# Four-layer convolution and attention kernel: tokens in raster order from the load on, and the mixer's stage order rewritten with three images in a turn

## Chip, cores and metric

The kernel runs on one NeuronCore of a Trainium2 chip. The metric is device time in microseconds of one execution; the time of a kernel is the median of several executions. TensorE (PE) has two clocks in these records, 1.2 and 2.4 GHz; a granted clock of 1.00 is 2.4 GHz.

## Reference

Sixteen images of 16 x 16 tokens with 96 channels pass through four layers: a window attention with an MLP, a convolutional mixer with an MLP, an attention over all 256 tokens with a quantised feed-forward part, a causal attention with a mixture of experts. Everything is float32. The change touches how tokens are laid out in the first layer, and the order of the work in the mixer of the second:

```python
h = _layernorm(x, n1_g, n1_b)
p = h @ w_in + b_in                                   # 96 -> 192 channels
local = depthwise 3x3 convolution of p
lr, rl = _ema_scan(local, axis=2), _ema_scan(local, axis=2, reverse=True)
tb, bt = _ema_scan(local, axis=1), _ema_scan(local, axis=1, reverse=True)
mixed = 0.25 * (lr + rl + tb + bt) + local
mixed = _layernorm(mixed, on_g, on_b)                 # over 192 channels
x = x + (mixed @ w_out + b_out)
```

The four scans are linear over the 256 tokens of an image, so the kernel does them, with the sum, as one product with a constant 256 x 256 matrix (`mixer`).

## The kernel before

X, the residual stream, stays in SBUF as 32 tiles of 128 tokens x 96 channels, two tiles an image. A tile is half an image (8 rows of 16 tokens). Until the mixer, the 128 tokens of a tile lie in window order: first the 64 tokens of the left 8 x 8 window, then those of the right one. From the mixer on they lie in raster order. The stages follow one another, each a block with one instruction stream for each engine, and semaphores between the streams. An engine runs its stream strictly in order, so the order in which the code calls its helpers is the order of the work.

**Load.** `x_loads` (line 344) issues for each group of four images and each window column eight DMAs of 8 partitions each; 64 in all, 8 of them on ScalarE's queue ahead of the first constants (`first`, line 384, of which the identity is the last) and the 16 loads of the bias table (line 386), 56 on SP's queue (line 350) ahead of the weights of the later layers (`k.late`, line 444). GpSimd's line 367 and TensorE's line 378 wait for the constants, and the first attention starts behind them.

**First attention.** TensorE transposes the normalised tiles (line 480), so that tokens become columns, and at the end transposes the outputs back (line 541), both in window order; the projection gives X in the same order.

**Mixer** (`conv_mixer`). Image n passes these steps; names are those of the functions in the code:
- tokens: GpSimd normalises (lines 156 to 165), TensorE transposes (L872), ScalarE copies out with scale and bias in two ACTIVATEs that also turn window order into raster order (L944);
- widen: 96 -> 192 channels (L879); ScalarE writes the result into two padded grids (L953);
- convolution: channels 0 to 127 on VectorE as nine dependent multiply-adds ("taps", L1019 for the first and L1022), channels 128 to 191 on TensorE (taps, L888), copied out by ScalarE as `acc1` (L968);
- conv_t: TensorE transposes both back to tokens (L901, L902), ScalarE copies out as `loc` (L976);
- mix: the product with the 256 x 256 matrix into bank 7 (L844);
- norm2: VectorE takes mean and variance (L984, L989), GpSimd the reciprocal root (L825, L827), VectorE normalises into Z (norm2b, L996);
- back: TensorE transposes Z (L854), ScalarE copies out with scale and bias as `zT` (zt, L936);
- out: TensorE projects 192 -> 96 (L865) and adds X itself in raster order by a product with a permutation matrix (`perm`, L863) into the same bank;
- residual: VectorE copies that to X (L178) and takes the statistics for the next MLP (L187, L193).

In turn n the engines run:
- TensorE: a warming product (`keep_warm`, L129, a bf16 product whose result is not used), tokens(n+1), out(n-2), mix(n-1), taps(n), widen(n+1), a warming product, back(n-1), a warming product, conv_t(n);
- ScalarE: tokens(n+1), acc1(n), grid(n+1), zt(n-1), loc(n);
- VectorE: taps 0 to 4 of n, residual(n-2), tap 5, norm2(n-1), taps 6 and 7, norm2b(n-1), tap 8;
- GpSimd: the normalisation for n+2, the reciprocal root for n-1.

conv_t(n) waits for all nine taps of n on VectorE, mix(n) for loc(n), norm2(n) for mix(n).

Of the kernel before, what the change touches and what calls it, by code (L numbers as in the profile page):

```python
# [22 lines left out]
ALU = mybir.AluOpType  # L23
# [3 lines left out]
P = 128  # L27
# [147 lines left out]
def add_new(dve, k, s, n, count, new, replace=False):  # L175

    x = tiles_of(k.X, n * count, count)
    (dve.tensor_copy(x, new) if replace else dve.tensor_tensor(x, x, new, ALU.add)).then_inc(s["x"], 1)  # L178
# [24 lines left out]
def add_and_stats(dve, k, s, n, count, new, replace=False):  # L203
    add_new(dve, k, s, n, count, new, replace)
    statistics(dve, k, s, n, count)
# [8 lines left out]
def setup(k, bank, a):  # L214
# [83 lines left out]
    k.perm = weight("perm", [P, P], a["perm"])  # L298
# [46 lines left out]
    def x_loads(eng, g, wx):  # L345

        for r in range(WS):
            p0 = wx * WTOK + r * WS
            src = a["x"].rearrange("b (y i) (v c) d -> v i c (b y) d", i=WS, c=WS)[wx, r]
            eng.dma_start(k.X[p0:p0 + WS, 8 * g:8 * g + 8, :], src[:, 8 * g:8 * g + 8, :]).then_inc(s[f"x{g}"], 16)  # L350

    def sync(sp):
        x_loads(sp, 0, 0)
        for g in range(1, 4):
            for wx in range(2):
                x_loads(sp, g, wx)
        sp.wait_ge(s["ones"], 1)
# [23 lines left out]
    def scalar(act):  # L381
        x_loads(act, 0, 1)
        for dst, src in first:
            act.dma_start(dst, src, allow_slow_non_contiguous=True).then_inc(s["w"], 16)
        for dst, src in table_loads:
            act.dma_start(dst, src, allow_slow_non_contiguous=True).then_inc(s["wr"], 16)
        act.wait_ge(s["w"], 16 * len(first))
        act.wait_ge(s["wr"], 16 * len(table_loads))
# [13 lines left out]
def image_stats(dve, k, s, i):  # L402

    dve.wait_ge(s[f"x{i // 4}"], 16 * 2 * WS)
    after(dve, s["mv"], i)
    for t in range(2):
        last = dve.bn_stats(k.stats[:, 6 + t, :], k.X[:, 2 * i + t, None, :])
    last.then_inc(s["bn"], 1)
    dve.wait_ge(s["bn"], i + 1)
    for t in range(2):  # L410
        last = dve.bn_aggr(k.MV[:, 2 * i + t, :], k.stats[:, 6 + t, :])
    last.then_inc(s["mv"], 1)


def window_attention(k, bank, begin):
# [3 lines left out]
    with ExitStack() as ctx:  # L419
# [19 lines left out]
        with nc.Block() as block:  # L439
# [33 lines left out]
            def _(pe):  # L473
                def tokens_t(n):

                    pe.wait_ge(s["y"], n + 1)
                    after(pe, s["hT"], n)
                    after(pe, s["x"], n - 4)
                    for t in range(2):
                        last = pe.transpose(bank[0][0:C, t * P:(t + 1) * P], k.Y[n % 2][:, t, :], k.ident[:])  # L480
                    last.then_inc(s["T"], 1)
# [55 lines left out]
                def outputs_t(n):  # L537
                    pe.wait_ge(s["a"], 2 * n + 2)
                    pe.wait_ge(s["hT"], min(n + 5, IMAGES))
                    for t in range(2):  # L540
                        last = pe.transpose(bank[0][0:C, t * P:(t + 1) * P], A[n % 2][:, t, :], k.ident[:])
                    last.then_inc(s["oT"], 1)
# [233 lines left out]
def raster(t, y):  # L776

    return t.rearrange("p (y i v c) -> p y v i c", y=2, i=WS, v=2)[:, y]


def conv_mixer(k, bank):

    nc = k.nc
    s = k.sems("cm", LN_SEMS + "z T hT in p taps acc1 conv ct loc mix bn2 ag2 va2 rs2 z2 zT zTe out diag init")
    with ExitStack() as ctx:
# [11 lines left out]
        v2, r2 = sb("v2", [P, 2, 1]), sb("r2", [P, 2, 1])  # L797
        Z = sb("z", [P, 2, CI])
        ZT = sb("zT", [P, 2, 2, P])

        with nc.Block() as block:
            @block.gpsimd
            def _(pool):
# [34 lines left out]
            def _(pe):  # L838
                def mix(n):
                    pe.wait_ge(s["loc"], n + 1)  # L840
                    after(pe, s["z2"], n)
                    for t in range(2):
                        for j in range(2):
                            last = pe.matmul(bank[7][:, t * CI:(t + 1) * CI], k.mixer[:, j, t * P:(t + 1) * P], loc[:, j, :],  # L844
                                             start=(j == 0), stop=(j == 1))
# [47 lines left out]
                def conv_t(n, slot):  # L893

                    keep_warm(pe, k, bank[4][:])
# [13 lines left out]
                for n in range(IMAGES + 2):  # L909
                    slot = n % 2  # L910
                    keep_warm(pe, k, bank[4][:])
# [12 lines left out]
                    if n < IMAGES:  # L924
                        conv_t(n, slot)

            @block.scalar
            def _(act):
# [11 lines left out]
                def tokens(n, slot):  # L940
                    act.wait_ge(s["T"], n + 1)
                    after(act, s["in"], n - 1)
                    for y in range(2):
                        last = act.activation(raster(k.hT[slot][:, 0:TOK], y), bank[0][0:C, y * P:(y + 1) * P].rearrange("p (v i c) -> p v i c", v=2, i=WS),  # L944
                                              ACT.Identity, bias=k.b3[:], scale=k.g3[:])
                    last.then_inc(s["hT"], 1)
# [14 lines left out]
                for n in range(IMAGES + 1):  # L961
                    slot = n % 2
                    if n + 1 < IMAGES:
                        tokens(n + 1, 1 - slot)
                    if n < IMAGES:
# [5 lines left out]
                    if n >= 1:  # L971
                        zt(n - 1)
# [6 lines left out]
            def _(dve):  # L979
                def norm2(n):  # L980
                    dve.wait_ge(s["mix"], n + 1)
                    after(dve, s["va2"], n)
                    for t in range(2):
                        last = dve.bn_stats(st2[:, t, :], bank[7][:, t * CI:(t + 1) * CI])  # L984
# [7 lines left out]
                def norm2b(n):  # L992
                    dve.wait_ge(s["rs2"], n + 1)
                    after(dve, s["zT"], n)
                    for t in range(2):
                        last = dve.tensor_scalar(Z[:, t, :], bank[7][:, t * CI:(t + 1) * CI], ag2[:, t, 0:1], r2[:, t, :], ALU.subtract, ALU.mult)  # L996
                    last.then_inc(s["z2"], 1)

                def residual(n):
                    dve.wait_ge(s["out"], n + 1)  # L1000
                    dve.wait_ge(s["xb"], n + 1)
                    add_and_stats(dve, k, s, n, 2, bank[6][:, 0:2 * C].rearrange("p (t c) -> p t c", t=2), replace=True)

                def body(n, slot, first, last):
# [18 lines left out]
                in_turn(IMAGES, body)  # L1023
                residual(IMAGES - 2)
                norm2(IMAGES - 1)
                norm2b(IMAGES - 1)
# [1172 lines left out]
def constants():  # L2199
# [7 lines left out]
    tok = np.arange(TOK).reshape(2, WS, 2, WS).transpose(0, 2, 1, 3).reshape(-1)  # L2207
# [4 lines left out]
        "perm": (tok[0:P, None] == np.arange(P)[None, :]).astype(f),  # L2212
# [23 lines left out]
```

## Time and profile before

| | us |
|---|---|
| median of 3 runs | 1274.22 (1272.11 to 1274.35) |
| the profiled execution | 1279.13 |
| its span | 1277.4 |

| engine | busy us | share of the span |
|---|---|---|
| TensorE matmul | 1150.9 | 90% |
| TensorE weight load | 786.9 | 62% |
| VectorE | 722.3 | 57% |
| ScalarE | 513.6 | 40% |
| GpSimd | 386.5 | 30% |

The profile is one execution recorded by the hardware; spans count from its first instruction. Busy shares are means over stages with different limits: the first attention runs from about 20 to 160 us, its MLP to 219, the mixer to 378, the second MLP to 435, the rest to the end. TensorE's granted clock is 0.954 over the whole.

### The profile page before, as it was taken

What the parts mean: (1) busy time and instruction counts of PE and PEld (TensorE: products, weight loads), DVE (VectorE), ACT (ScalarE), POOL (GpSimd) and SP (SyncE); (2) the same over time, 40 slices, a digit from 0 to 9 for tenths busy, and PEclk for the clock granted to TensorE, in tenths of its full rate; (3) what the DMA queues carried; (4) which work ended last, traced back from release to release, by engine and by line L of the source; (5) the groups of instructions that cost most, each with busy time, mean ns of one, the idle gap of its engine ahead of it and who ended that gap; (6) DMA issues with size and microseconds to landing.
All of it is one profiled execution on the core that took longest, in us unless ns stands there. A gap on an engine that the chain in (4) does not pass through costs nothing. (4 is left out here: it accounts for less than half of the span.)

```text
span 1277.4 us, 23732 instructions
## 1 busy us (share of the span) xinstructions
PE 1150.9 (90%) x8911; PEld 786.9 (62%) x8911; DVE 722.3 (57%) x2035; ACT 513.6 (40%) x839; POOL 386.5 (30%) x584
## 2 busy tenths in 40 slices
PE   4999988999979799999999996788898887999998
PEld 2677655666646566767676664465445444577776
DVE  3899633777743266666666675475556556333232
ACT  1666532444413244333433330545344322445543
POOL 3666463544336311110101111434001000263522
PEclk9999999899989899999999997888899997999999
DMA  4500000000000000000000000000000000000000
GB/s 89 97 18 2 2 1 0 1 1 1 1 1 1 1 1 1 1 1 1 1 1 1 1 1 1 0 1 1 2 2 2 1 2 1 1 13 7 13 7 13
DMA packets 28923, 9.38 MB, mean 7 GB/s; under 512 B 26961, under 2 KB 28816, under 8 KB 28816
## 3 DMA queue, kind: packets, MB, share of 16 engines
q1 hardware_dynamic: 25760, 7.02, 2.7%
q8 instruction: 69, 1.13, 0.4%
q10 hardware_dynamic: 3056, 0.92, 0.3%
q14 instruction: 38, 0.31, 0.1%
HBM read 6.36 MB, written 1.57 MB: 6 GB/s over the span
## 5 line engine op out<-in xcount | busy, mean ns | idle before, releaser
L156 POOL TENSOR_TENSOR ln_v<-MV,eps 128x2 f32<-128x2 f32 (+3 forms) x81 | 16.4, 202 | 420.5 <-PE bank L1144 245.8
L1206 ACT ACTIVATE fa_e<-bank 128x1024 f32<-128x1024 f32 x64 | 65.5, 1024 | 158.5 <-PE bank L1114 158.5
L2009 PEld LDWEIGHTS bank<-e_w,ex_G 128*128 128x128 f32 x768 | 90.6, 192 | 14.4 <-issue 14.1
L2124 DVE SCALAR_TENSOR_TENSOR X<-bank,ex_L,X 128x96 f32<-128x96 f32 x128 | 31.7, 310 | 114.5 <-PE bank L2009 108.8
L1258 DVE TENSOR_REDUCE fa_z<-bank 128x4 f32<-128x1024 f32 x64 | 77.9, 1216 | 26.3 <-PE bank L1096 24.7
L2001 PE MATMUL bank<-hT,e_w 96*128 96x512 f32 x192 | 91.3, 612 | 0.0
L2009 PE MATMUL bank<-e_w,ex_G 128*128 128x96 f32 x768 | 90.0, 274 | 0.0
L2052 ACT ACTIVATE ex_G<-bank,e_b 128x512 f32<-128x512 f32 x96 | 64.4, 687 | 63.0 <-PE bank L2001 60.2
L1856 DVE TENSOR_REDUCE ca_z<-bank 128x2 f32<-128x256 f32 x96 | 48.9, 552 | 50.2 <-PE bank L1583 50.0
L1114 PE MATMUL bank<-fa_a,fa_b 64*128 64x256 f32 x512 | 73.4, 406 | 1.1 <-DVE fa_a L1265 1.1
L1127 PE MATMUL bank<-fa_e,fa_v 128*64 128x256 f32 x512 | 71.2, 400 | 1.1 <-ACT fa_e L1206 1.1
L159 POOL TENSOR_TENSOR ln_r<-ln_v,minus_half 128x2 f32<-128x2 f32 (+3 forms) x81 | 71.8, 887 | 0.0
L1774 ACT ACTIVATE ca_e<-bank 128x768 f32<-128x768 f32 x48 | 38.9, 811 | 80.7 <-PE bank L1583 80.7
L1022 DVE SCALAR_TENSOR_TENSOR cm_acc<-cm_g,k_conv,cm_acc 128x256 f32<-128x256 f32 x128 | 64.7, 505 | 3.0
L1096 PE MATMUL bank<-fa_b,fa_a 64*128 64x256 f32 x512 | 66.0, 376 | 0.1
L1955 POOL TENSOR_TENSOR ex_tmp<-e_b,ex_L 128x384 f32<-128x384 f32 x8 | 6.7, 835 | 190.5 <-DVE ex_L L2112 190.5
L1114 PEld LDWEIGHTS bank<-fa_a,fa_b 64*128 64x128 f32 x512 | 44.7, 189 | 29.4 <-issue 24.6
L178 DVE TENSOR_TENSOR X<-X,bank 128x192 f32<-128x192 f32 (+2 forms) x56 | 23.7, 429 | 67.3 <-PE bank L730 43.0
L468 POOL TENSOR_TENSOR wa_s<-wa_s,wa_mx 128x768 f32<-128x768 f32 x32 | 47.1, 1473 | 46.9 <-DVE wa_mx L666 46.9
L1569 PE MATMUL bank<-ca_b,ca_a 16*128 16x256 f32 (+1 forms) x384 | 48.0, 369 | 14.3 <-DVE ca_a L1865 13.8
L163 POOL TENSOR_TENSOR Y<-Y,ln_r 128x192 f32<-128x192 f32 (+3 forms) x81 | 56.2, 694 | 10.9
L1265 DVE TENSOR_TENSOR fa_a<-fa_a,bank 128x256 f32<-128x256 f32 x64 | 26.9, 421 | 56.3 <-PE bank L1104 56.3
(252 smaller groups left out, 2620.3 us busy)
## 6 DMA issues: line engine op xcount, KB each, us to landing
out_tokens<-X SPq DMA_DIRECT2D x8, 192.0 KB, 2.1
X<-in_x SPq DMA_DIRECT2D x56, 24.0 KB
e_w<-in_L_ffn_w SPq DMA_DIRECT2D x2, 576.0 KB
bias0r<-in_L_conv_rpb_table ACTq DMA_DIRECT2D x16, 24.0 KB
m0w<-in_L_conv_mlp_w SPq DMA_DIRECT2D x2, 144.0 KB
m1w<-in_L_conv_w SPq DMA_DIRECT2D x2, 144.0 KB
f_w<-in_L_ffn_W SPq DMA_DIRECT2D x2, 142.5 KB
mixer<-in_mixer SPq DMA_DIRECT2D x1, 256.0 KB
```

The lines of the kernel that those rows point to most:

```text
L159: pool.tensor_tensor(r, v, k.minus_half[:, 0:count, :], ALU.pow).then_inc(s["rstd"], 1)
L163: pool.tensor_tensor(y, y, r.broadcast_to([P, count, C]), ALU.mult).then_inc(s["y"], 1)
L1022: dve.scalar_tensor_tensor(out=o, in0=src, scalar=kk, in1=o, op0=ALU.mult, op1=ALU.add).then_inc(s["conv"], 1)
L1096: last = pe.matmul(bank[b + i][:, c * TOK:(c + 1) * TOK], A[n % 2][rows, p, c * P:(c + 1) * P], B[n % 2][rows, p, :], start=True, stop=True)
L1114: last = pe.matmul(bank[b + i][:, c * TOK:(c + 1) * TOK], B[n % 2][rows, p, c * P:(c + 1) * P], A[n % 2][rows, p, :], start=True, stop=True)
L1127: last = pe.matmul(bank[4 + v % 2][64 * i:64 * i + 64, 0:TOK], V[n % 2][:, c, 2 * p + i, :], E[v % 2][:, i, c, :], start=(c == 0), stop=(c ...
L1206: act.activation(E[v % 2][:], k.banks[:, b:b + 2, :].rearrange("p i (c q) -> p i c q", c=2), ACT.Exp).then_inc(s["exp"], 1)
L1258: dve.tensor_reduce(Z[v % 2][:].rearrange("p c (i d) -> p i c d", i=2)[:, :, :, D2], k.banks[:, b:b + 2, :].rearrange("p i (c q) -> p i c ...
L1856: last = dve.tensor_reduce(dst, k.banks[:, 2 * p:2 * p + 2, c * P:(2 * c + 1) * P], AX.X, ALU.max, negate=True)
L2001: pe.matmul(bank[v % NB][:], k.ew1[:, e, j * P:(j + 1) * P], k.hT[slot][:], start=True, stop=True).then_inc(s["up"], 1)
L2009: last = pe.matmul(bank[4 + e % 2][:, t * C:(t + 1) * C], G[e % 2][:, j, t * P:(t + 1) * P], k.ew2[:, e, j, :], start=(j == 0), stop=(j == ...
L2052: act.activation(G[e % 2][:, j, :], bank[(KH * e + j) % NB][:], ACT.Gelu, bias=k.eb1[:, e, j:j + 1]).then_inc(s["gelu"], 1)
```

## The change

- X is loaded with one DMA an image, in raster order; 2 of the 16 are issued by ScalarE, 14 by SP. The transposes of the first attention write their columns in window order, those of its output read in window order and write in raster order. The permutation matrix and its two products go; the residual is added by VectorE.
- In the mixer the normalisation after the mixing moves from VectorE to ScalarE (`normalised`, two ACTIVATEs with scale and bias from columns); GpSimd makes the bias in two more small operations. The result of the mixing has two banks (7 and 4) by turns. back, zt and out of an image come a turn later than before; residual comes in the third turn after the taps.
- The order within a turn changes on all engines, the last turn runs two turns after the last taps, and the warming products of the mixer go.

```diff
-    def x_loads(eng, g, wx):
-        for r in range(WS):
-            p0 = wx * WTOK + r * WS
-            src = a["x"].rearrange("b (y i) (v c) d -> v i c (b y) d", i=WS, c=WS)[wx, r]
-            eng.dma_start(k.X[p0:p0 + WS, 8 * g:8 * g + 8, :], src[:, 8 * g:8 * g + 8, :]).then_inc(s[f"x{g}"], 16)
+    def x_load(eng, image):
+        src = a["x"].rearrange("b (y i) w d -> (i w) (b y) d", i=WS)
+        eng.dma_start(k.X[:, 2 * image:2 * image + 2, :], src[:, 2 * image:2 * image + 2, :]).then_inc(s[f"x{image // 4}"], 16)
     def sync(sp):
-        x_loads(sp, 0, 0)
-        for g in range(1, 4):
-            for wx in range(2):
-                x_loads(sp, g, wx)
+        for image in (0, 2) + tuple(range(4, IMAGES)):
+            x_load(sp, image)
     def scalar(act):
-        x_loads(act, 0, 1)
+        for image in (1, 3):
+            x_load(act, image)
...
-                        last = pe.transpose(bank[0][0:C, t * P:(t + 1) * P], k.Y[n % 2][:, t, :], k.ident[:])
+                        windows = bank[0][0:C, t * P:(t + 1) * P].rearrange("p (v i c) -> p i v c", v=2, i=WS)
+                        last = pe.transpose(windows, k.Y[n % 2][:, t, :], k.ident[:])
...
-                        last = pe.transpose(bank[0][0:C, t * P:(t + 1) * P], A[n % 2][:, t, :], k.ident[:])
+                        rows = bank[0][0:C, t * P:(t + 1) * P].rearrange("p (i v c) -> p v i c", i=WS, v=2)
+                        last = pe.transpose(rows, A[n % 2][:, t, :], k.ident[:])
...
+        mixed = (bank[7], bank[4])
...
                     pool.tensor_tensor(v2[:], ag2[:, :, 1:2], k.eps[:, 0:2, :], ALU.add).then_inc(s["va2"], 1)
-                    pool.wait_ge(s["va2"], n + 1)
+                    pool.tensor_scalar(m2[:, :, 0], ag2[:, :, 0], -1.0, 0.0, ALU.mult, ALU.add).then_inc(s["va2"], 1)
+                    pool.wait_ge(s["va2"], 2 * n + 2)
                     pool.tensor_tensor(r2[:], v2[:], k.minus_half[:, 0:2, :], ALU.pow).then_inc(s["rs2"], 1)
+                    pool.wait_ge(s["rs2"], n + 1)
+                    pool.tensor_tensor(o2[:], m2[:], r2[:], ALU.mult).then_inc(s["of2"], 1)
...
                 def mix(n):
                     pe.wait_ge(s["loc"], n + 1)
-                    after(pe, s["z2"], n)
+                    after(pe, s["z2"], n - 1)
...
                 def out(n):
                     pe.wait_ge(s["zTe"], n + 1)
                     after(pe, s["x"], n)
-                    pe.wait_ge(s["xb"], n + 1)
                     for t in range(2):
-                        o = bank[6][:, t * C:(t + 1) * C]
-                        pe.matmul(o, k.perm[:], k.X[:, bass.ds(n * 2 + t, 1), :], start=True, stop=False)
                         for j in range(2):
-                            last = pe.matmul(o, ZT[0:part[j], j, t, :], k.wout[0:part[j], j, :], start=False, stop=(j == 1))
+                            last = pe.matmul(bank[6][:, t * C:(t + 1) * C], ZT[0:part[j], j, t, :], k.wout[0:part[j], j, :],
+                                             start=(j == 0), stop=(j == 1))
...
                 for n in range(IMAGES + 2):
                     slot = n % 2
-                    keep_warm(pe, k, bank[4][:])
                     if n + 1 < IMAGES:
                         tokens(n + 1, 1 - slot)
                     if n >= 2:
-                        out(n - 2)
+                        back(n - 2)
+                    if n < IMAGES:
+                        taps(n, slot)
                     if 1 <= n <= IMAGES:
                         mix(n - 1)
-                    if n < IMAGES:
-                        taps(n, slot)
                     if n + 1 < IMAGES:
                         widen(n + 1, 1 - slot)
-                    if 1 <= n <= IMAGES:
-                        back(n - 1)
+                    if n >= 2:
+                        out(n - 2)
                     if n < IMAGES:
                         conv_t(n, slot)
...
+                def normalised(n):
+                    act.wait_ge(s["of2"], n + 1)
+                    after(act, s["zT"], n)
+                    for t in range(2):
+                        last = act.activation(Z[:, t, :], mixed[n % 2][:, t * CI:(t + 1) * CI], ACT.Identity, bias=o2[:, t, :], scale=r2[:, t, :])
+                    last.then_inc(s["z2"], 1)
...
-                for n in range(IMAGES + 1):
+                for n in range(IMAGES + 2):
                     slot = n % 2
+                    if n >= 2:
+                        normalised(n - 2)
                     if n + 1 < IMAGES:
                         tokens(n + 1, 1 - slot)
+                    if n >= 2:
+                        zt(n - 2)
...
                     if n + 1 < IMAGES:
                         widened(n + 1, 1 - slot)
-                    if n >= 1:
-                        zt(n - 1)
...
                     for tap in range(9):
-                        if tap == 5 and n >= 2:
-                            residual(n - 2)
-                        if tap == 6 and not first:
+                        if tap == 1 and n >= 3:
+                            residual(n - 3)
+                        if tap == 4 and not first:
                             norm2(n - 1)
-                        if tap == 8 and not first:
-                            norm2b(n - 1)
```

The two `keep_warm` lines in front of back and conv_t go as well, `norm2b` goes, ScalarE's tokens become one ACTIVATE of 256 columns, and after the last turn VectorE runs residual(13), norm2(15), residual(14), residual(15).

## Rows read from the trace of the kernel before

**Rows 1.** Windows: busy time of each engine in a stretch, granted clock, DMA share, GB/s.

```profile
core 0: us, PE busy (x) PEld busy (x) DVE busy (x) ACT busy (x) POOL busy (x), PEclk, DMA share, GB/s
233.00:300.00 67.00, 60.94 (x386) 44.21 (x384) 53.78 (x152) 28.06 (x67) 27.16 (x52) 1.00 0.01 1
```

**Rows 2.** Timeline of one turn of the mixer; start, duration, engine, line.

```profile
300.37 0.87 DVE L996 TENSOR_SCALAR cm_z<-bank,cm_ag,cm_r 128x192 f32<-128x192 f32 x2 [0.60 <-POOL cm_r L827]
...
301.14 0.48 DVE L1022 SCALAR_TENSOR_TENSOR cm_acc<-cm_g,k_conv,cm_acc 128x256 f32<-128x256 f32 x1
301.29 0.39 PEld L854 LDWEIGHTS bank<-ident,cm_z 128*128 128x128 f32 x4 [1.52 <-DVE cm_z L996]
...
301.78 0.14 PEld L901 LDWEIGHTS bank<-ident,cm_acc 128*128 128x128 f32 x1
301.92 2.38 DVE L1022 SCALAR_TENSOR_TENSOR cm_acc<-cm_g,k_conv,cm_acc 128x256 f32<-128x256 f32 x4
...
302.90 0.47 ACT L976 ACTIVATE cm_loc<-bank 128x384 f32<-128x384 f32 x1
303.05 0.30 PEld L863 LDWEIGHTS bank<-X,perm 128*128 128x128 f32 x2
...
305.05 1.57 PE L844 MATMUL bank<-cm_loc,mixer 128*128 128x192 f32 x8
...
306.55 1.52 PE L888 MATMUL bank<-cm_g,cm_diag 128*64 128x256 f32 x12
306.67 0.62 DVE L984 BATCH_NORM_STATS2 cm_st<-bank 128x6 f32<-128x192 f32 x2
...
307.56 0.45 DVE L1022 SCALAR_TENSOR_TENSOR cm_acc<-cm_g,k_conv,cm_acc 128x256 f32<-128x256 f32 x1
```

**Rows 3.** Timeline: conv_t of images 0 and 15, taps without GpSimd beside them.

```profile
232.25 0.14 PEld L901 LDWEIGHTS bank<-ident,cm_acc 128*128 128x128 f32 x1 [0.96 <-DVE cm_acc L1022]
...
354.74 2.05 DVE L1022 SCALAR_TENSOR_TENSOR cm_acc<-cm_g,k_conv,cm_acc 128x256 f32<-128x256 f32 x4
...
363.12 0.14 PEld L901 LDWEIGHTS bank<-ident,cm_acc 128*128 128x128 f32 x1
```

**Rows 4.** Groups by form, 240 to 366 us; busy us, mean ns, idle before.

```profile
L944 ACT ACTIVATE hT<-bank,w_b,w_g 96x128 f32<-96x128 f32 x26 | 10.3, 452 | 0.0
L936 ACT ACTIVATE cm_zT<-bank,on_b,on_g 128x256 f32<-128x256 f32 x15 | 8.5, 566 | 7.2 <-PE bank L854 7.2
```

**Rows 5.** Timeline of the mixer's tail, after the last mixing.

```profile
370.99 1.11 PE L854 MATMUL bank<-ident,cm_z 128*128 128x128 f32 x4 [2.81 <-DVE cm_z L996]
...
373.21 0.74 PE L863 MATMUL bank<-X,perm 128*128 128x96 f32 x2 [0.68 <-ACT cm_zT L936]
...
374.97 0.74 PE L863 MATMUL bank<-X,perm 128*128 128x96 f32 x2
...
376.85 0.36 DVE L178 COPY X<-bank 128x192 f32<-128x192 f32 x1 [5.92 <-PE bank L865]
```

**Rows 6.** Timeline of the kernel's start; the queues' own rows are the issues.

```profile
0.74 3.05 ACTq L350 DMA_DIRECT2D X<-in_x  x8
0.75 19.60 SPq L350 DMA_DIRECT2D X<-in_x  x56
...
8.70 0.45 ACTq L384 DMA_DIRECT2D ident<-in_ident  x1
...
12.86 0.37 POOL L367 TENSOR_SCALAR bv_wide<-ones,w_bv 96x128 f32<-96x128 f32 x1 [9.80 <-DMA ident<-in_ident]
```

**Rows 7.** Taps in the mixer's first turn (timeline); windows of 3 us in later stages.

```profile
227.10 2.83 PE L888 MATMUL bank<-cm_g,cm_diag 128*64 128x256 f32 x12
...
910.00:913.00 3.00, 1.44 (x20) 0.93 (x19) 1.50 (x3) 0.81 (x1) 0.00 (x0) 1.00 0.01 3
913.00:916.00 3.00, 3.00 (x36) 1.47 (x32) 1.10 (x3) 0.81 (x1) 0.00 (x0) 0.62 0.00 0
...
1038.00:1041.00 3.00, 1.70 (x21) 1.06 (x21) 1.48 (x4) 0.81 (x1) 0.00 (x0) 1.00 0.00 0
```

More of the change, by code:

```diff
@@ L172, in next_first_step, with add_new @@
     normalise(pool, k, s, steps, count, k.Y[0][:, 0:count, :], bias, steps, 0)
-def add_new(dve, k, s, n, count, new, replace=False):
+def add_new(dve, k, s, n, count, new):
     x = tiles_of(k.X, n * count, count)
-    (dve.tensor_copy(x, new) if replace else dve.tensor_tensor(x, x, new, ALU.add)).then_inc(s["x"], 1)
+    dve.tensor_tensor(x, x, new, ALU.add).then_inc(s["x"], 1)
 def statistics(dve, k, s, n, count, unrolled=True):
@@ L200, in statistics, with add_and_stats @@
     dve.tensor_copy(tiles_of(k.MV, n * count, count), k.aggr[:, 0:count, :]).then_inc(s["mv"], 1)
-def add_and_stats(dve, k, s, n, count, new, replace=False):
-    add_new(dve, k, s, n, count, new, replace)
+def add_and_stats(dve, k, s, n, count, new):
+    add_new(dve, k, s, n, count, new)
     statistics(dve, k, s, n, count)
@@ L297, in setup @@
     k.bout = row("b_out", a["L1_conv_b_out"])
-    k.perm = weight("perm", [P, P], a["perm"])
     k.mixer = weight("mixer", [P, 2, TOK], a["mixer"].rearrange("(j p) t -> p j t", p=P))
@@ L402, in image_stats @@
 def image_stats(dve, k, s, i):
-    dve.wait_ge(s[f"x{i // 4}"], 16 * 2 * WS)
+    dve.wait_ge(s[f"x{i // 4}"], 16 * 4)
     after(dve, s["mv"], i)
@@ L773, in _ @@
                 residual(steps - 1)
-def raster(t, y):
-    return t.rearrange("p (y i v c) -> p y v i c", y=2, i=WS, v=2)[:, y]
 def conv_mixer(k, bank):
     nc = k.nc
-    s = k.sems("cm", LN_SEMS + "z T hT in p taps acc1 conv ct loc mix bn2 ag2 va2 rs2 z2 zT zTe out diag init")
+    s = k.sems("cm", LN_SEMS + "z T hT in p taps acc1 conv ct loc mix bn2 ag2 va2 rs2 of2 z2 zT zTe out diag init")
     with ExitStack() as ctx:
@@ L796, in conv_mixer @@
         st2, ag2 = sb("st2", [P, 2, 6]), sb("ag2", [P, 2, 2])
-        v2, r2 = sb("v2", [P, 2, 1]), sb("r2", [P, 2, 1])
+        v2, r2, m2, o2 = (sb(f"{name}2", [P, 2, 1]) for name in "vrmo")
         Z = sb("z", [P, 2, CI])
         ZT = sb("zT", [P, 2, 2, P])
+        mixed = (bank[7], bank[4])
         with nc.Block() as block:
@@ L840, in mix @@
                     pe.wait_ge(s["loc"], n + 1)
-                    after(pe, s["z2"], n)
+                    after(pe, s["z2"], n - 1)
                     for t in range(2):
                         for j in range(2):
-                            last = pe.matmul(bank[7][:, t * CI:(t + 1) * CI], k.mixer[:, j, t * P:(t + 1) * P], loc[:, j, :],
+                            last = pe.matmul(mixed[n % 2][:, t * CI:(t + 1) * CI], k.mixer[:, j, t * P:(t + 1) * P], loc[:, j, :],
                                              start=(j == 0), stop=(j == 1))
@@ L893, in conv_t @@
                 def conv_t(n, slot):
-                    keep_warm(pe, k, bank[4][:])
                     pe.wait_ge(s["conv"], 9 * (n + 1))
@@ L910, in _ @@
                     slot = n % 2
-                    keep_warm(pe, k, bank[4][:])
                     if n + 1 < IMAGES:
@@ L942, in tokens @@
                     after(act, s["in"], n - 1)
[L943 to L946, printed above, removed]
+                    act.activation(k.hT[slot][:, 0:TOK], bank[0][0:C, 0:TOK], ACT.Identity, bias=k.b3[:], scale=k.g3[:]).then_inc(s["hT"], 1)
+                def normalised(n):
[4 more added lines that the diff above has]
+                    last.then_inc(s["z2"], 1)
                 def widened(n, slot):
@@ L981, in norm2 @@
                     dve.wait_ge(s["mix"], n + 1)
-                    after(dve, s["va2"], n)
+                    after(dve, s["va2"], 2 * n)
                     for t in range(2):
-                        last = dve.bn_stats(st2[:, t, :], bank[7][:, t * CI:(t + 1) * CI])
+                        last = dve.bn_stats(st2[:, t, :], mixed[n % 2][:, t * CI:(t + 1) * CI])
                     last.then_inc(s["bn2"], 1)
@@ L990, in norm2 @@
                     last.then_inc(s["ag2"], 1)
[L992 to L997, printed above, removed]
                 def residual(n):
@@ L1001, in residual @@
                     dve.wait_ge(s["xb"], n + 1)
-                    add_and_stats(dve, k, s, n, 2, bank[6][:, 0:2 * C].rearrange("p (t c) -> p t c", t=2), replace=True)
+                    add_and_stats(dve, k, s, n, 2, bank[6][:, 0:2 * C].rearrange("p (t c) -> p t c", t=2))
                 def body(n, slot, first, last):
@@ L1023, in _ @@
                 in_turn(IMAGES, body)
+                residual(IMAGES - 3)
+                norm2(IMAGES - 1)
                 residual(IMAGES - 2)
-                norm2(IMAGES - 1)
-                norm2b(IMAGES - 1)
                 residual(IMAGES - 1)
@@ L2206, in constants @@
     mixer = np.eye(TOK) + 0.25 * (np.kron(eye, scan) + np.kron(scan, eye))
-    tok = np.arange(TOK).reshape(2, WS, 2, WS).transpose(0, 2, 1, 3).reshape(-1)
     return {
@@ L2211, in constants @@
         "stack2": np.tile(np.eye(CI - P, dtype=f), (2, 1)),
-        "perm": (tok[0:P, None] == np.arange(P)[None, :]).astype(f),
         "headmask": (np.arange(C)[:, None] // D0 % (H0 // 3) == np.arange(H0 // 3)[None, :]).astype(f),
```

## Prediction

> **What bounds the kernel now.** The window view comes first, stage by stage: all of the arithmetic that the change touches lies in the mixer, and there TensorE is busy 60.9 of 67 us and VectorE 53.8, the clock at 2.4 GHz [rows 1]. With both that full, shares decide nothing; the turn has to be read in the timeline, engine against engine. The reader should follow one loop in it [rows 2]. The last tap of image n ends on VectorE at 301.62; 0.16 us later TensorE starts the transposes of the convolution (conv_t, 301.78); ScalarE copies them out until 303.37 (loc); TensorE meanwhile does the tokens of the next image and the output projection, and at 305.05 starts the mixing, which ends at 306.62; VectorE starts the statistics at 306.67 and is back at its taps at 307.56. Behind that come two taps, GpSimd's reciprocal root (VectorE waits 0.60 us for it), VectorE's normalisation (0.87) and the last tap, and the next conv_t. Nothing in this loop has slack over about 1 us. conv_t starts fifteen turns apart at 232.25 and 363.12: 130.87 us, 8.72 us a turn [rows 3].
>
> **What the change moves in the turn.** In turn n TensorE now runs: tokens(n+1), back(n-2), taps(n), mix(n-1), widen(n+1), out(n-2), conv_t(n). ScalarE runs: z(n-2) (the normalisation, two ACTIVATEs), tokens(n+1), zt(n-2), acc1(n), the grid of n+1, loc(n). VectorE runs: tap 0, residual(n-3), taps 1 to 3, statistics of n-1, taps 4 to 8. I lay it out from conv_t(n-1) at time 0, with the durations of before.
>
> - loc(n-1) ends at 303.37 - 301.78 = 1.59 [rows 2]. z(n-2) stands behind it in ScalarE's queue, though its inputs were ready a turn ago. 128x192 with scale and bias from columns does not occur; the nearest forms are 96x128 at 452 ns and 128x256 at 566 ns [rows 4], so 0.51 each. One ACTIVATE starts about 0.1 before the one in front ends (two of 0.45 take 0.80), so the pair takes 0.92 and ends at 1.59 - 0.10 + 0.92 = 2.41. Bounds of the pair: 0.80 (two of the smaller form) and 1.02 (two of the larger).
> - TensorE has its tokens done at about 1.1 and waits. back(n-2) starts at 2.45 and gives way after 0.39 of weight loads [rows 2]: taps(n) start at 2.84. They take 1.52, of which, as between mix and taps now, 0.07 overlaps: mix(n-1) starts at 4.29 and ends at 4.29 + 1.57 = 5.86 [rows 2].
> - VectorE's tap 0, residual and taps 1 to 3 need about 0.4 + 1.3 + 1.65, so it stands at the statistics from 3.2 on, and waits some 2.7 us for the mixing. Statistics start at 5.91 and hold it for 307.56 - 306.67 = 0.89: 6.80.
> - Five taps remain. Four took 2.38 beside GpSimd's work and 2.05 without it [rows 2, 3], 0.51 to 0.60 each; five cost 2.56 to 2.98, taken 2.75: 9.55. conv_t(n) starts 0.16 later: **9.71 us a turn**, with 9.2 to 10.1 as bounds when all the small terms fall one way.
>
> All of it is one closed chain (conv_t, loc, z, back, taps, mix, statistics, five taps), so work taken off beside it brings nothing. VectorE loses z, 0.87 a turn, and gains about 0.1 (adding in place of copying): cover, as it now waits 2.7. TensorE loses the two permutation products (out is now 2.00 us for six products, a third of them permutations) and all three or four warming products: out ends at 5.86 + 1.0 + 1.35 = 8.2, and TensorE then waits 1.5 for the taps. GpSimd gains two operations of some 0.2 to 0.35, beside a wait of several us. The tokens' one ACTIVATE for two (0.3 less) is beside the wait for taps. The second bank for the mixing removes a wait that nobody stood at.
>
> The first turn has no z and no back: tokens done at 1.1, taps at 1.2, mix ends at 4.22, then 0.05 + 0.89 + 2.75 + 0.16 give 8.07. Fourteen more at 9.71 are 135.9. Together 144.0 against 130.87: **+13.1 us** (9.2 a turn: +5.8; 10.1: +18.5).
>
> **Tail.** Now 376.85 - 363.12 = 13.73 from the last conv_t to the last residual [rows 3, 5]. After: mix(15) behind back(14) without taps between ends at 4.41; statistics to 5.3; GpSimd's four small operations about 1.6; z(15) 0.92: 7.8; back at 1.2 GHz 1.11; zt 1.0; out twice 1.76 [rows 5] less its third for the permutation, 2.4: 12.4. **-1.3.** The head of the stage gains 0.3 from the tokens.
>
> **Load.** ScalarE issues eight X loads in 3.05 us before the constants; the identity is issued at 8.70 and GpSimd, TensorE and everything behind wait for it until 12.86 [rows 6]. Now there are two X loads. At 0.38 each the other six are 2.3 us. The loads are four times as large, and SP's 14 are out by about 6 us rather than at 20.35 [rows 6], so more is in flight when the identity travels. The nearest row for that is the identity itself, 4.1 us from issue to use under the present traffic; bounds: another 1.5 us off that, or 4 us on top. Taken: **-2.0**, range -3.5 to +2. SP's weight loads start some 14 us earlier and are needed after 160 us: nothing. The Trainium skill (Trainium Kernel Development and Optimization, Key Constraints) says that loads of the SP and ACT queues run on the same 16 engines and interleave, so that several issuers save issue time only; by it the transfer gains nothing and the saving is the 2.3 us of issue at most. No row separates the two.
>
> In the first attention the transposes write their columns in window order; that they cost more appears in no row. A transpose takes a slot of 0.1 us (0.39 for four [rows 2]); 64 of them at double price would be 6 us. Taken at nothing: the number of columns is the same.
>
> The Trainium skill (ScalarE: Activation LUTs, What ACT_TABLE_LOAD costs) gives an ACTIVATE 186 ns and 0.833 ns an element, 93 ns more for each column operand, and an overlap of 93 ns between neighbours. For z that is 532 ns, a pair of 0.97 us: an estimate from the page, against VectorE's 0.87 now. It speaks against moving z, and by it the fifteen turns would be 0.7 us longer still. The rows that it can be held to agree: 566 measured for 128x256 against 585.
>
> **Clock.** From the end of out (8.2) to the next taps (9.71 + 2.84 = 12.55) TensorE has 4.3 us with only conv_t, tokens and back in them, some 1.4 us of short operations, and the warming products that stood there are gone. The rows show what such thin stretches were followed by, and it is not always the same: after 3 us with TensorE busy 1.44 came a spell at 1.2 GHz, through 3 us with 1.70 it stayed at 2.4 [rows 7], and after the 2.81 us wait in the tail back came at 1.2 [rows 5]. So this cost is open. Taps take 2.83 at 1.2 GHz and 1.52 at 2.4 [rows 7, 2]; with a piece of the mixing a fall costs 1.3 to 1.7 us of the chain. The clock comes back once the dense part of the turn has run, so I take a fall in one turn of three, between never and always: 5 times 1.4, **+7** (0 to 22).
>
> **Sum.** 13.1 - 1.3 - 0.3 - 2.0 + 7 = +16.5. The profiled execution took 1279.1 (span 1277.4), so it would take 1295.6; it lies 4.9 above the median of 1274.2, and against the median I forecast **1290**.
>
> **The rivals.**
>
> *The clock holds.* The loop is the same and no fall is paid: +9.5, 1283.7 (1279 to 1287 by the turn's bounds). For it: in the mixer now TensorE waits over 1 us each turn and the clock never falls [rows 1, 2]; against: warming products fill those waits.
>
> *The clock falls every turn.* 14 times 1.6: +22 in place of +7, 1306. If it fell and stayed, TensorE's whole part of the chain (conv_t, back, taps, mix, 4.2 us) would double: 14 times 4.2, near 1340. Against that: the dense part has brought the clock back each time, as at 913 [rows 7].
>
> *Faster: the wait for z is not paid.* Place: back(n-2) on TensorE. Price: if z were there when TensorE comes (1.1 and not 2.45), the mixing would end 1.35 sooner and the turn be 8.36; 8.07 + 14 x 8.36 = 125.1, -5.8, with tail, head and load -9.4 and no low clock: 1265. It decides from a mixing that ends before 4.9 after conv_t, where the turn is 8.75. For it: z's inputs are ready early and it has a bank of its own. Against it: z can't pass loc in ScalarE's queue, and loc needs conv_t.
>
> *It comes out even.* A turn at 9.2, no low clock and the full gain of the load: +5.8 - 1.6 - 3.5, 1275.
>
> **How the numbers follow.** Forecast 0.45; clock holds 0.27; falls every turn 0.11, stays low 0.05; even 0.05; faster 0.07. The range leaves out the faster, the even and the stay-low case: 1278 to 1308. A measurement can tell about 0.2%, 2.5 us, from no change: slower 0.88, same 0.05, faster 0.07.
>
> **What would show it.** In the profile of after: conv_t starts 9.7 us apart (10 to 10.5 where the clock fell); VectorE waits about 2.7 us a turn for the mixing before the statistics, and hardly at all for GpSimd or out; TensorE waits about 1.3 us for z before back and 1.5 for the taps before conv_t; identity in use at about 10.8; granted clock in the mixer below 1.00 in some slices. I am wrong on the main term if VectorE reaches the statistics after the mixing has ended, or if turns are under 9.2 us.

## The result and the profile after

| | before | after |
|---|---|---|
| median, us (4 runs each) | 1273.16 (1269.46 to 1274.35) | 1311.91 (1310.65 to 1312.31) |
| span of the profiled execution, us | 1277.4 | 1310.5 |
| its TensorE clock | 0.954 | 0.932 |
| conv_t of image 0, of image 15, us | 232.25, 363.12 | 227.64, 395.27 |
| between the two, us | 130.87 | 167.63 |
| of it at 1.2 GHz, us | 0 | 64.9 in 14 spells |

The change makes the kernel slower: ratio 1.0308, 95% interval 1.0284 to 1.0332. That is 38.7 us on the medians, where 16.5 was forecast; 1311.91 lies above the range as well. The direction was right, and so was the closed loop that the prediction laid out; the term for the clock was much too small.

The two spans differ by 33.1 us, and four stretches make them up: the start until conv_t(0) -4.6, the fifteen turns +36.8, the tail +0.5, everything behind +0.4. (The rest of the 38.7: the profiled execution of before lay 6.0 above the median of its four runs, that of after 0.4.) The stages behind the mixer took 893 to 901 us in the twelve kernels shown here, with the same code in them, so below the turns are compared first and whole times second.

The mixer in the view of waits of after, 226 to 400 us (who waits for whom: us in total, times, longest):

```profile
DVE cm_st L982 <- PE bank L841: 69.1, 15, 6.0
...
PEld bank L894 <- DVE cm_acc L1011: 25.7, 16, 3.1
...
PE bank L894 <- DVE cm_acc L1011: 22.6, 16, 2.7
...
PE bank L850 <- ACT cm_z L941: 19.8, 15, 1.5
```

All three waits that the prediction named are there. TensorE waits 1.3 us a turn for z (L850) and 1.5 for the taps (L894); VectorE waits for the mixing (L982), but 4.6 a turn and not 2.7. The timeline of one turn of after shows why:

```profile
292.12 0.14 PEld L894 LDWEIGHTS bank<-ident,cm_acc 128*128 128x128 f32 x1 [1.46 <-DVE cm_acc L1011]
...
292.95 0.49 ACT L974 ACTIVATE cm_loc<-bank 128x384 f32<-128x384 f32 x1 [2.13 <-PE bank L895]
...
293.46 0.91 ACT L941 ACTIVATE cm_z<-bank,cm_o,cm_r 128x192 f32<-128x192 f32 x2
...
295.06 2.83 PE L882 MATMUL bank<-cm_g,cm_diag 128*64 128x256 f32 x12
...
297.82 1.80 PE L841 MATMUL bank<-cm_loc,mixer 128*128 128x192 f32 x8
...
299.66 0.63 DVE L982 BATCH_NORM_STATS2 cm_st<-bank 128x6 f32<-128x192 f32 x2 [4.34 <-PE bank L841]
...
300.56 2.54 DVE L1011 SCALAR_TENSOR_TENSOR cm_acc<-cm_g,k_conv,cm_acc 128x256 f32<-128x256 f32 x5
...
303.14 0.14 PEld L894 LDWEIGHTS bank<-ident,cm_acc 128*128 128x128 f32 x1 [1.46 <-DVE cm_acc L1011]
```

The loop is the forecast one: conv_t 292.12, loc, z until 294.37, back, taps at 295.06, mixing at 297.82, statistics at 299.66, five taps, conv_t at 303.14. But the taps take 2.83 us and the mixing 1.80, against 1.52 and 1.57 in [rows 2]. Windows over the same turn give the clock (the last three numbers are clock, DMA share, GB/s):

```profile
289.00:292.00 3.00, 1.83 (x11) 1.33 (x9) 2.75 (x10) 1.30 (x3) 2.14 (x6) 1.00 0.00 0
292.00:294.40 2.40, 1.00 (x8) 0.75 (x8) 2.17 (x9) 1.43 (x4) 2.27 (x4) 1.00 0.00 0
294.40:297.90 3.50, 3.47 (x17) 1.70 (x17) 0.89 (x2) 1.44 (x3) 0.12 (x1) 0.57 0.02 5
...
299.60:303.10 3.50, 2.25 (x13) 1.70 (x11) 3.19 (x10) 1.30 (x3) 2.22 (x6) 1.00 0.00 0
```

TensorE stands for 1.46 us, does 1.00 us of short transposes in 2.4, and the clock then falls to 1.2 GHz under back and the taps, which are on the chain. It is back by the end of the mixing, the two waits come again, and it falls again. Over 67 us of the mixer, where [rows 1] has TensorE busy 60.94 at 1.00:

```profile
233.00:300.00 67.00, 50.59 (x255) 35.66 (x256) 35.23 (x100) 26.77 (x59) 27.16 (x54) 0.80 0.00 1
```

The turns after the first take 10.8 to 12.6 us in place of 8.72 (nine of 10.8 to 11.1, five of 12.2 to 12.6; in the long ones the mixing is wholly at 1.2 GHz too, 2.5 to 2.7 us).

### The profile page after: what moved, and what is told of

Same layout as the page of the kernel before. It is cut to its first block and busy times, and to the rows that moved or that the text cites. A ratio compares the mean times of both kernels' runs of the same rounds, so it can differ in the third digit from the quotient of the medians.

```text
span 1310.5 us, 23469 instructions
## 1 busy us (share of the span) xinstructions
PE 1155.4 (88%) x8797; PEld 789.9 (60%) x8797; DVE 707.7 (54%) x2003; ACT 525.5 (40%) x855; POOL 397.6 (30%) x616
## 3 DMA queue, kind: packets, MB, share of 16 engines
HBM read 6.29 MB, written 1.57 MB: 6 GB/s over the span
## 5 line engine op out<-in xcount | busy, mean ns | idle before, releaser
L178 DVE TENSOR_TENSOR X<-X,bank 128x192 f32<-128x192 f32 (+2 forms) x72 | 29.1, 409 | 74.3 <-PE bank L728 43.0
L163 POOL TENSOR_TENSOR Y<-Y,ln_r 128x192 f32<-128x192 f32 (+3 forms) x81 | 56.3, 695 | 10.9
L157 POOL TENSOR_TENSOR Y<-X,MV 128x192 f32<-128x192 f32 (+5 forms) x81 | 58.2, 718 | 0.0
```

## The experiments

Theory A: the closed chain costs about 9 us by itself, and the rest is the clock, which falls in the two waits. Rivals: the clock is a side effect and the chain alone costs the whole; or the loss comes from one part of the change (z on ScalarE, raster order, the lost warming products). All edits are of the kernel after unless said. The turns come from the timelines (starts of conv_t), the ratios from 10 runs each where no other number stands, against 13 to 25 runs of before on the same chip.

### Three warming products back in their old places (e1_warm, 4 runs)

```diff
+                    keep_warm(pe, k, mixed[(n + 1) % 2][:])        # ahead of tokens
+                        keep_warm(pe, k, mixed[(n + 1) % 2][:])    # ahead of back
+                        keep_warm(pe, k, mixed[n % 2][:])          # ahead of conv_t
```

> The changed kernel with the three warming products of the old mixer put back at the same three places (ahead of tokens, of back and of conv_t), written into whichever of the two mixing banks is free. They run while TensorE waits anyway. Theory (low clock in every turn adds 1.5 us to a chain of 9.7): the clock stays at 2.4 GHz, conv_t starts fall from 11.2 to 9.7 us apart, 144 us from the first to the last in place of 168, and the kernel takes about 1288. Rival (the chain itself is longer than laid out, the clock is a bystander): 1305 to 1312, with turns over 11 us at a granted clock of 1.00, or with the clock falling in spite of the products.

Measured: 1301.9 us, 1.0222 (1.0195 to 1.0248). 154.67 us from first to last conv_t, 44.4 of it at 1.2 GHz in 11 spells. The clock was expected to stay up and the fifteen turns to take 144 us: it did not. The three turns without a fall took 9.42 to 9.43. So three products of some 0.2 us don't hold the clock, and they bring 13 us in the mixer by sparing three falls and shortening others. That they are gone is a small part of the loss; what is large is the waits that they no longer fill.

### Products until both waits are full (e6_warm_more)

```diff
+                        keep_warm(pe, k, mixed[(n + 1) % 2][:], 5)   # ahead of back
+                        keep_warm(pe, k, mixed[n % 2][:], 6)         # ahead of conv_t
```

> The changed kernel with more warming products than three: five (of 0.21 us each) ahead of back, in the wait for z, and six ahead of conv_t, in the wait for the taps. Theory (the chain at 2.4 GHz is 9.4 to 9.7 us, the rest of the changed kernel's 11.2 is low clock; three products a turn, as in the last experiment, filled too little of the waits): the clock stays at 2.4 GHz through the mixer, every turn is 9.4 to 9.7, fifteen 139 to 144, the kernel 1284 to 1290. Rival (warming products can't hold the clock here, or lengthen the chain themselves): turns of 10.2 or more, 1300.

Measured: 1278.0 us, 1.0038 (1.0014 to 1.0061), the clock at 1.00 from first to last conv_t. Its windows and one turn:

```profile
233.00:300.00 67.00, 64.06 (x389) 42.26 (x385) 43.28 (x123) 32.55 (x72) 32.02 (x63) 1.00 0.00 1
```

```profile
290.75 1.57 PE L841 MATMUL bank<-cm_loc,mixer 128*128 128x192 f32 x8
...
292.36 0.63 DVE L984 BATCH_NORM_STATS2 cm_st<-bank 128x6 f32<-128x192 f32 x2 [2.75 <-PE bank L841]
...
293.26 2.54 DVE L1013 SCALAR_TENSOR_TENSOR cm_acc<-cm_g,k_conv,cm_acc 128x256 f32<-128x256 f32 x5
...
295.85 0.14 PEld L894 LDWEIGHTS bank<-ident,cm_acc 128*128 128x128 f32 x1 [0.39 <-DVE cm_acc L1013]
...
297.18 0.91 ACT L943 ACTIVATE cm_z<-bank,cm_o,cm_r 128x192 f32<-128x192 f32 x2
...
298.15 0.66 PE L850 MATMUL bank<-ident,cm_z 128*128 128x128 f32 x4 [0.22 <-ACT cm_z L943]
```

This is the chain of the change at full clock, with no work of the kernel altered: 139.90 us, 7.47 for the first turn and 9.43 to 9.44 for all others but one. It splits the 36.8 us of after: **+9.0 for the chain, +27.7 for the clock**. That the clock is a cause and not a side effect is shown by this run: with eleven products that have no use the median is 33.9 us lower, and the turns without a fall in e1 above and e8 below take the same 9.43.

### Products in the wait for z alone (e8_warm_z_only, 4 runs)

```diff
+                        keep_warm(pe, k, mixed[(n + 1) % 2][:], 5)   # ahead of back
```

> The changed kernel with only the five products ahead of back; the wait before conv_t stays empty. If the thin stretch counts as a whole, from the end of out to the next taps, filling its second half saves most of the falls: turns near 9.5 mostly, 1288 to 1295. If the wait ahead of conv_t makes the clock fall by itself, turns stay at 10.5 to 11 and the kernel at 1300 to 1310.

Measured: 1291.5 us, 1.0147 (1.0106 to 1.0189), 37.5 us at 1.2 GHz in 11 spells, of which the first was already running when the stage began. TensorE in two turns, in the second of which the clock falls:

```profile
281.23 1.24 PE L129 MATMUL bank<-causal,identb 128*128 128x512 bf16 x5
...
289.82 0.33 PE L894 MATMUL bank<-ident,cm_acc 128*128 128x128 f32 x1 [1.30 <-DVE cm_acc L1012]
...
291.06 2.34 PE L129 MATMUL bank<-causal,identb 128*128 128x512 bf16 x5
293.20 0.82 PE L850 MATMUL bank<-ident,cm_z 128*128 128x128 f32 x4
293.95 1.52 PE L882 MATMUL bank<-cm_g,cm_diag 128*64 128x256 f32 x12
```

With only the wait for the taps open (1.30), the clock still falls, right behind conv_t; it hits the products and back, is over when the taps start, and such a turn takes 10.6 against 9.43. So the wait for the taps alone brings falls, in 10 turns. The wait for z alone was not tried with nothing else changed, but in e3 and e10 below it is the only one left, and there the clock falls in 10 turns too.

### Before without its warming products (e5_before_cold)

Edit of the kernel before: its three `keep_warm` calls in the mixer are removed.

> The kernel before with the three warming products of the mixer taken out and nothing else. If warming products are what kept the clock up in the old turn, the clock falls in some turns, and each fall costs 1 to 1.5 us: 1280 to 1290. If the old turn is dense enough by itself (its waits are 1.0 to 1.3 us in one place), the clock stays at 2.4 GHz and the kernel is within 3 us of 1274.

Measured: 1279.2 us, 1.0056 (1.0028 to 1.0083). Windows of its mixer:

```profile
228.00:260.00 32.00, 27.09 (x146) 19.77 (x146) 21.92 (x61) 13.66 (x33) 12.50 (x24) 0.84 0.01 1
260.00:300.00 40.00, 35.02 (x223) 25.84 (x224) 32.26 (x94) 15.73 (x38) 15.35 (x30) 1.00 0.00 1
```

In the profiled execution the clock falls twice (turns of 11.31 and 10.47) and then holds to the end at 8.76 a turn with no product at all. There the old order keeps the clock by its own work; without the products the fifteen turns take 3.9 us more, all at the start of the stage (medians: 5.9). Together with e1, where the clock falls in 11 turns with the three products back, this makes the lost products a small part of the falls in the new order.

### Raster order alone (e4_raster_only)

The kernel after (load, transposes, tokens in one ACTIVATE, adding in place of the permutation) with the mixer in its old order:

```diff
 # relative to before
-                    pe.wait_ge(s["xb"], n + 1)
-                        pe.matmul(o, k.perm[:], k.X[:, bass.ds(n * 2 + t, 1), :], start=True, stop=False)
```

> Raster order alone: loads, transposes, no permutation products and one ACTIVATE for the tokens as in the changed kernel, but the mixer's stage order, normalisation on VectorE and warming products as before. Theory: the load gives 2.9 us, and since out stands between conv_t and mix in the old order, the permutation products gone take 0.66 off each of fifteen turns: 1273.2 - 2.9 - 0.3 - 9.9 = 1260. Rival (the old turn has another bound right behind): the load's gain only, about 1270.

Measured: 1264.4 us, 0.9918 (0.9899 to 0.9938): this half of the change is a gain of 10.9. conv_t(0) at 228.29 (-4.0), then 8.31 a turn against 8.76, 124.91 in all (-6.0), with the clock at 1.00, and the tail 1.7 shorter. The removed permutation products and the shorter token copy lie on the old chain, and 0.45 a turn is what they cost there (0.66 had been expected). In the kernel after they stand beside the chain, where TensorE and ScalarE wait anyway, so the same 0.45 should be worth nothing; this is read from the loop, no run shows it.

### z an image earlier on ScalarE (e7_z_early)

```diff
-                    if n >= 2:
-                        normalised(n - 2)        # first in the turn, so behind loc(n - 1)
+                    if 1 <= n <= IMAGES:
+                        normalised(n - 1)        # ahead of loc(n)
```

> The changed kernel with z(n-1) placed ahead of loc(n) at the end of ScalarE's turn, in place of behind it in the next turn; TensorE's order and VectorE's stay. It is the case of the forecast's rival in which the wait for z is not paid. Theory: back follows tokens without a wait, the mixing ends near 4.5 after conv_t in place of 5.9, a turn is 8.4 us at 2.4 GHz; fifteen 125 us and 1269 for the kernel if the clock holds, 1280 to 1290 if it falls in most turns. Rival (z is not on the chain, the wait for it is only where a wait for something else shows): no change beside the changed kernel's 1312.

Measured: 1271.3 us, 0.9984 (0.9961 to 1.0007). back no longer waits, a turn without a fall takes 7.91 (8.4 expected), one with a fall 9.50 to 9.54; 8 spells, 27.3 us at 1.2 GHz, 131.69 in all. The only wait that TensorE has left is the one for the taps (view of waits, 240 to 335 us):

```profile
PE bank L894 <- DVE cm_acc L1011: 14.6, 11, 1.7
```

So the place in ScalarE's queue cost 9.43 - 7.91 = 1.5 us a turn, by one in-order position and not by more work.

### The statistics behind tap 8 (e3_stats_late)

```diff
-                        if tap == 4 and not first:
+                        if tap == 8 and not first:
```

> The changed kernel with the statistics (norm2) ahead of tap 8 in place of tap 4; TensorE's order stays. Theory: the mixing still ends near 5.9 after conv_t (2.4 GHz), but only one tap is left behind it, so conv_t is held by TensorE's own queue: 2.45 + 0.39 + 1.45 + 1.5 + 1.0 + 1.35 = 8.2 us a turn if the clock holds, 123 us for fifteen and 1267 for the kernel; with the clock falling in each turn 9.5 and 1286. Rival (the statistics' place is not what VectorE's wait costs, the low clock is): as the changed kernel, 1305 or more.

Measured: 1277.4 us, 1.0031 (1.0008 to 1.0055). VectorE does four more taps before it waits for the mixing: 8.07 without a fall, mostly 9.59 to 9.66 with one, 134.36 in all, 34.1 us at 1.2 GHz in 10 spells. Here TensorE waits for z alone (same view and stretch), and the clock falls all the same:

```profile
PE bank L850 <- ACT cm_z L941: 13.0, 10, 1.3
```

### The mixing ahead of the taps (e10_mix_after_back, e2_mix_first in 4 runs, e9_mix_z_early in 4 runs)

TensorE's order in the turn is edited; e9 has the edit of e7 too:

```diff
 # e10, e9: back(n - 2), mix(n - 1), taps(n)
 # e2:      mix(n - 1), back(n - 2), taps(n)
 # after:   back(n - 2), taps(n), mix(n - 1)
```

> The changed kernel with mix(n-1) between back(n-2) and taps(n): ahead of the taps, but still behind the wait for z. Theory (of the chain of 9.4 us, the taps' 1.45 and the wait for z, 1.5, can be taken off one by one): the mixing ends near 4.4 after conv_t, VectorE's chain would allow 8.0, TensorE's own queue behind the wait for z 2.4 + 0.4 + 1.5 + 1.45 + 1.0 + 1.35 = 8.1: a turn of 8.1 at 2.4 GHz as with the late statistics, 9.6 where the clock falls, 1265 to 1280. Rival (only the place behind the taps costs, z does not): 7.2 a turn as with the mixing first, 1248.

> The changed kernel with one move on TensorE: mix(n-1) ahead of back(n-2) and taps(n). Theory (VectorE stands at tap 4 because the mixing is behind z, back and taps): the mixing ends at 1.6 + 1.57 = 3.2 after conv_t, as VectorE gets to its statistics, whose wait goes from some 4.5 us to under 0.5; a turn is then bound by VectorE's own work, 7.2 to 7.7 us, TensorE has no long wait left and the clock holds. Fifteen turns 112 us in place of 168: 1256. Rival (clock alone is to blame, the place of the mixing matters little): a turn of 9 us or more, 1280 or above.

> Both at once: z(n-1) ahead of loc(n) on ScalarE, and TensorE's order tokens, back, mix, taps, widen, out, conv_t. Back fills the wait for loc. Theory: TensorE has no wait left but 0.1 for loc; its own work, 6.9 us, is the turn against 7.17 with the mixing first, fifteen 104 in place of 108.6 and 1244 for the kernel. Rival (ScalarE's queue now delays loc, because z stands ahead of it and waits for GpSimd): 7.2 or more, no gain, 1248 to 1255.

| kernel | median, ratio to before (95%) | first to last conv_t | a turn | at 1.2 GHz |
|---|---|---|---|---|
| e10 | 1277.2, 1.0006 (0.9981 to 1.0032) | 134.40 | 8.07, with a fall 9.5 to 9.7 | 34.1, 10 spells |
| e2 | 1247.8, 0.9798 (0.9766 to 0.9829) | 108.62 | 7.17 | 6.9, at the start only |
| e9 | 1243.1, 0.9741 (0.9697 to 0.9784) | 101.96 | 6.82 | 0 |

Windows of e2 and of e9:

```profile
240.00:300.00 60.00, 57.10 (x373) 43.18 (x372) 49.08 (x153) 37.93 (x84) 35.01 (x75) 1.00 0.01 1
```

```profile
240.00:300.00 60.00, 59.53 (x392) 45.23 (x392) 52.44 (x158) 38.95 (x89) 38.33 (x79) 1.00 0.01 1
```

and the turn of e9:

```profile
289.38 0.14 PEld L894 LDWEIGHTS bank<-ident,cm_acc 128*128 128x128 f32 x1 [0.23 <-DVE cm_acc L1011]
...
290.79 1.52 PE L841 MATMUL bank<-cm_loc,mixer 128*128 128x192 f32 x8
...
292.24 1.51 PE L882 MATMUL bank<-cm_g,cm_diag 128*64 128x256 f32 x12
...
292.50 0.62 DVE L982 BATCH_NORM_STATS2 cm_st<-bank 128x6 f32<-128x192 f32 x2
```

The taps of TensorE are needed by nobody in a hurry (ScalarE copies them out as they end, after 1.8 us of idling, and conv_t comes 2.4 us later), the mixing by VectorE at once. Put behind the mixing they fill TensorE while VectorE does the statistics and five taps, which is where after had its wait of 1.46. With z out of the way as well TensorE is busy 59.53 of 60 us: it is the bound by its own work, the clock did not fall in any turn, and all the work that the change took off TensorE at last counts. e9 is 31.6 us faster than before and 69 faster than after, with the changed kernel's operations and no warming product.

## Why the prediction was wrong in size

Term by term, measured less forecast on the spans: the chain -4.1, the clock +20.7, the tail +1.8, load and head -2.3, the stages behind +0.4. Together this is the distance from +16.5 to +33.1. The miss is the clock; the other terms together took 4.2 off it.

*The chain: right, slightly too long.* Laid out from conv_t as in the prediction, with the times of e6 beside the forecast: z ends at 2.24 (2.41), back 2.30 (2.45), taps 2.89 (2.84), mixing 4.33 (4.29), statistics 5.94 (5.91), the last taps begin at 6.84 (6.80), conv_t at 9.43 (9.71). Every point up to the last taps agrees within 0.2. The five taps took 2.54, where 2.75 had been taken from bounds of 2.56 to 2.98. The ACTIVATE pair for z took 0.91 against 0.92 taken (the estimate of 0.97 by the Trainium skill, ScalarE: Activation LUTs, What ACT_TABLE_LOAD costs, is 0.06 above what the trace shows). The term was +13.1 and measured +9.0. The first turn took 7.47, not 8.07.

*The clock: the step that failed.* "So I take a fall in one turn of three ... 5 times 1.4, +7." The stretch itself was read rightly: 4.2 us from the end of out to the taps, with only short products in it. What was wrong is the frequency: the clock fell in each of the 14 turns. One in three had no row of its own; it was a choice between never and always, since the rows showed both outcomes [rows 5, 7]. What makes a stretch fall or not stays open: with only one of the two waits left, every turn had the same gap and the clock fell in 8 to 10 of the fifteen (e7; e3, e8, e10). The price was too low as well: 27.7 / 14 = 2.0 us a fall. The nine shorter turns cost 1.4 to 1.6 each, close to the 1.4 taken and to the falls of e3, e7 and e10 (about 1.5). In the five long ones, which the forecast did not have, the mixing is at 1.2 GHz along with the taps (2.51 to 2.71 against 1.57), and they cost 2.7 to 2.9. The rival "falls every turn" had the right frequency at 1.6 and a chance of 0.11: with 2.0 in it, +28, and the chain as measured, it is what happened.

*Tail: -1.3 forecast, +0.5 measured.* The last mixing ran at 1.2 GHz behind two more waits; back and out behind it did so in before too [rows 5]:

```profile
398.34 2.64 PE L841 MATMUL bank<-cm_loc,mixer 128*128 128x192 f32 x8
...
404.49 1.12 PE L850 MATMUL bank<-ident,cm_z 128*128 128x128 f32 x4 [2.14 <-ACT cm_z L941]
...
406.70 2.75 PE L858 MATMUL bank<-w_out,cm_zT 128*128 128x96 f32 x8 [1.10 <-ACT cm_zT L928]
```

With the products of e6 the last mixing, back and out are all at 2.4 GHz and the tail takes 11.1 in place of 14.2, so 3.2 us of it are the clock; the mixing there:

```profile
374.33 1.47 PE L841 MATMUL bank<-cm_loc,mixer 128*128 128x192 f32 x8
```

*Load and head: -2.3 forecast, -4.6 measured until conv_t(0).* The start of after, to be read against [rows 6]:

```profile
0.74 1.02 ACTq L347 DMA_DIRECT2D X<-in_x  x2
...
6.86 0.49 ACTq L380 DMA_DIRECT2D ident<-in_ident  x1
...
11.55 0.37 POOL L362 TENSOR_SCALAR bv_wide<-ones,w_bv 96x128 f32<-96x128 f32 x1 [8.50 <-DMA ident<-in_ident]
```

The identity was in use at 11.55 in place of 12.86, 1.3 earlier. It was issued 1.8 earlier, not 2.3, since each of the larger loads took 0.5 us to issue in place of 0.38; from issue to use it took 4.7 in place of 4.2. That half microsecond is not clearly the larger loads: e5, with the loads of before, took 3.4 from issue to use, the nine kernels of other experiments with the new loads 4.3 to 5.0. The Trainium skill (Trainium Kernel Development and Optimization, Key Constraints) says that loads from several queues run on the same 16 engines, so that spreading them saves issue time only; the trace agrees in so far as issue time is all that was gained. The warming products behind it then ran faster; before first, after second:

```profile
13.88 7.24 PE L129 MATMUL bank<-causal,identb 128*128 128x512 bf16 x20
20.95 0.38 PE L480 MATMUL bank<-ident,Y 128*96 128x128 f32 x2
```

```profile
12.57 5.70 PE L129 MATMUL bank<-causal,identb 128*128 128x512 bf16 x20
18.10 0.38 PE L477 MATMUL bank<-ident,Y 128*96 128x128 f32 x2
```

which makes -2.85 at the first attention. Of this at most the 1.3 is the load's: the time of these twenty products differs from kernel to kernel, and e5, with the loads of before, took 5.89 for them and began the attention at 18.86. Nor is the rest until conv_t(0) the change's to claim: that start lies between 227.4 and 231.8 in the kernels that share its load, and at 228.6 in e5, which does not. So the -4.6 is in large part luck; no run separates the load's share.

*The strided transposes: nothing, as taken.* In the first attention, 28 to 160 us, TensorE is busy 127.07 us against 127.45 before, with the clock at 1.00 against 0.99.

*The rival "faster: the wait for z is not paid"* was dismissed for after, rightly, as z can't pass loc in the queue. But it named what a one-line edit brings: 8.36 a turn forecast for it, 7.91 in e7.

The signs looked for: conv_t 9.7 apart (10 to 10.5 with a fall) was 9.43, and 10.8 to 12.6 with one; the waits of TensorE were as named; VectorE's was 2.75 at full clock (e6) as named and 4.6 a turn in the trace of after (4.34 in the turn shown), since the mixing comes later by what the taps take longer.

Left open: why the falls in after differ in length (turns of 10.9 and 12.2), why one wait of 1.3 us a turn brings falls in e3, e7, e8 and e10 while the old order holds the clock with a wait of 1.0 and no product (e5), and how many products between three and eleven would have been enough.

## What to carry to other kernels

Lay a reordered turn out as one loop over the engines: here a step moved in front of another in two queues (z behind loc, taps ahead of the mixing) made two waits of 1.3 to 1.5 us, while each engine had less work than before. Then put first, on each engine, what another engine stands waiting for. When new waits leave TensorE with only short transposes for some microseconds in every turn, price a fall of the clock in most turns if not in each (in 8 to 14 of the fifteen here), and in whatever products follow on the chain; a variant with products until the waits are full tells at once how much of a loss is the clock.

## What the runs showed of the hardware

- The clock can fall and come back once a turn, over a whole stage: 14 spells and 64.9 us of 167.6 at 1.2 GHz, with no single wait of TensorE over 1.5 us in most turns. One wait of 1.3 us a turn was enough for falls in 10 of fifteen turns (e3, e8, e10) or in 8 (e7).
- Three products of 0.2 us a turn changed that little (11 spells), five in one of the waits hardly more (10, and one that began ahead of the stage), eleven in both ended it (0).
- The old order held 1.00 without any such product once two falls were past (e5, the profiled execution): whether they are needed depends on the order around them.
- Twenty warming products at the start took 5.70 us in one kernel and 7.24 in the other: read as the clock having risen after fewer of them. In e5, with the start of the slower one, they took 5.89: this is no effect of the change.
